# Attention kernel with maxima computed ahead: the first maximum of a plain part moves between the two units of scores

## The reference

```python
q, k, v = (proj(Wq), proj(Wk), proj(Wv))          # 8 heads of 64, 2 sequences of 1024
dots = jnp.einsum('bhqd,bhkd->bhqk', q, k) * scale
attn = jax.nn.softmax(dots, axis=-1)
out = jnp.einsum('bhqk,bhkd->bhqd', attn, v)
```

## Time and profile before

| what | value |
|---|---|
| time, median of 3 runs (lowest to highest) | 388.75 us (388.74 to 388.98) |
| the profiled execution's own time | 388.68 us |
| its span | 386.9 us |
| TensorE busy, matmuls | 378.4 us (98%) |
| TensorE busy, weight loads | 221.9 us (57%) |
| VectorE busy | 274.1 us (71%) |
| ScalarE busy | 276.6 us (72%) |
| GpSimd busy | 293.9 us (76%) |

### The profile page before, as it was taken

One profiled execution on the slowest core, in us unless ns is written; L12 is line 12 of the kernel. 1 busy time (PEld: TensorE's weight loads), 2 busy tenths in 40 slices (PEclk: granted clock), 3 DMA queues, 4 the chain that ended last, 5 costly groups with the idle time before them and its releaser, 6 DMA issues.

```text
span 386.9 us, 6735 instructions
## 1 busy us (share of the span) xinstructions
PE 378.4 (98%) x2368; PEld 221.9 (57%) x2368; DVE 274.1 (71%) x485; ACT 276.6 (72%) x396; POOL 293.9 (76%) x145
## 2 busy tenths in 40 slices
PE   8989999999999999999999999999999999999995
PEld 7856544544555445445544544454456644599995
DVE  6997777787877787777777777877784545766223
ACT  3566656568878887987788687969885589347753
POOL 3080486949999999999999999999999699800021
PEclk9999999999999999999999999999999999999999
DMA  4001002101122041104010710261053105000001
GB/s 138 16 0 36 19 3 56 56 0 56 41 74 56 3 101 12 55 3 110 3 55 5 217 57 1 50 171 57 4 129 93 55 1 160 6 2 15 14 30 54
DMA packets 28245, 19.46 MB, mean 50 GB/s; under 512 B 21264, under 2 KB 23696, under 8 KB 28212
## 3 DMA queue, kind: packets, MB, share of 16 engines
q1 hardware_dynamic: 27636, 18.05, 17.9%
q10 hardware_dynamic: 576, 0.98, 0.8%
HBM read 17.72 MB, written 1.17 MB: 49 GB/s over the span
## 4 chain that ended last, share of the span: by engine, by line
PE 93%; DVE 4%; issue 1%; ACT 1%; DVEq 0%
PE psum L693 31%; PE psum L682 24%; PE psum L620 11%; PE psum L608 6%; PE psum L629 4%; PE psum L737 4%; PE psum L748 3%; PE psum L584 2%; PE psum L704 2%; DVE half_maxes L1127 1%; PE psum L559 1%; PE psum L645 1%; PE psum L647 1%; PE psum L771 1%; PE psum L533 1%
## 5 line engine op out<-in xcount | busy, mean ns | idle before, releaser
L1131 DVE TENSOR_REDUCE half_maxes<-psum 128x1 f32<-128x512 f32 x232 | 148.9, 683 | 26.1 <-PE psum L620 24.5
L894 ACT ACTIVATE probs<-psum 128x1024 f32<-128x1024 f32 x128 | 124.8, 1022 | 54.5 <-PE psum L682 54.1
L693 PE MATMUL psum<-probs,v_all 128*64 128x512 f32 x512 | 123.7, 604 | 0.0
L1360 POOL TENSOR_TENSOR sums<-sums,probs 128x1024 f32<-128x1024 f32 x31 | 74.2, 2395 | 3.7 <-ACT probs L894 3.7
L1360 POOL TENSOR_TENSOR odd_sum<-odd_sum,probs 128x1024 f32<-128x1024 f32 x31 | 74.2, 2395 | 0.0
L693 PEld LDWEIGHTS psum<-probs,v_all 128*64 128x64 f32 x512 | 31.2, 136 | 62.4 <-issue 42.3
L1179 DVE TENSOR_SCALAR psum<-max_plane 128x512 f32<-128x512 f32 (+1 forms) x55 | 43.0, 790 | 31.7 <-ACT probs L894 31.7
L1360 POOL TENSOR_TENSOR sums<-probs 128x1024 f32<-128x1024 f32 x16 | 38.0, 2375 | 27.5 <-ACT probs L894 27.0
L620 PE MATMUL psum<-k_round,q_round 64*128 64x512 f32 x256 | 57.7, 449 | 0.6 <-DVE half_maxes L1131 0.5
L620 PEld LDWEIGHTS psum<-k_round,q_round 64*128 64x128 f32 x256 | 24.1, 183 | 53.5 <-DVE half_maxes L1131 42.9
L682 PE MATMUL psum<-q_round,k_round 64*128 64x512 f32 x256 | 52.4, 404 | 0.1
(11 more groups left out here) (131 smaller groups left out, 450.7 us busy)
## 6 DMA issues: line engine op xcount, KB each, us to landing
max_plane<-rows_scratch SPq DMA_DIRECT2D x16, 512.0 KB, 3.9
inv_sb<-inv_scratch SPq DMA_DIRECT2D x14, 256.0 KB, 5.4
max_rows_of<-maxes SPq DMA_DIRECT2D x128, 0.5 KB, 2.0
v_all<-in_fc SPq DMA_DIRECT2D x4, 512.0 KB, 6.9
fc_late<-in_fc SPq DMA_DIRECT2D x4, 512.0 KB, 6.8
out_h<-probs SPq DMA_DIRECT2D x7, 128.0 KB, 1.8
v_all<-in_w ACTq DMA_DIRECT2D x3, 256.0 KB, 3.6
woT<-in_wo SPq DMA_DIRECT2D x1, 256.0 KB, 3.5
```

The lines of the kernel that those rows point to most:

```text
L693: last = pe.matmul(out_bank[head_rows(h), :], v_all[:, s, kc, head_rows(h)], probs[unit(s, kc, half) % TILES][:, h, :], start=(kc == 0), s ...
L894: last = act.activation(probs[u % TILES][:, heads, :], source, ACT.Exp, scale=SCALE)
L1131: dve.reduce_max(half_maxes[:, h, qc, keys:keys + 1], slot[:, h, :], AX.X).then_inc(maxed, 1)
L1360: pool.tensor_tensor(chain[:, :, :], first[:, :, :], probs[kc][:, :, :], ALU.add).then_inc(own, 1)
```

## The change

In a plain part (two maxima, or none) the first maximum stands between the two units instead of ahead of them, and the second unit's share stands behind the second maximum instead of ahead of it. The lists for the first two parts, for parts with three maxima and for the first part of the last step stay as they are.

```diff
@@ -128,7 +128,7 @@
     elif (s, part) == (STEPS - 1, 0):
         items = maxes[:1] + [first, second] + maxes[1:] + shares[0] + shares[1]
     else:
-        items = maxes[:1] + [first] + shares[0] + [second] + shares[1] + maxes[1:]
+        items = [first] + maxes[:1] + [second] + shares[0] + maxes[1:] + shares[1]
     items += beside_values(s, part)
     items += [("fill", *u) for u in following if u in SCALAR_FILLED]
     if turn > 0:
```

## The result

The changed kernel takes 409.48 us (median of 4 runs, 409.41 to 409.53) against 388.75 us: a ratio of 1.0533, 95% interval 1.0518 to 1.0549. It is 20.7 us slower; the prediction was 411.3 us. The span grew from 386.9 to 407.7 us.

The account below looks back on a forecast made before the run. The prediction took TensorE's own queue, and the releases it waits for, to bound plain parts. Its terms, 14.9 + 4.1 + 2.4 + 1.0 + 0.25 = 22.6 us, on 388.75 us gave 411.3 us, range 404.5 to 416 us.

Parts of the forecast that it names:

- What is moved: In 49 plain parts, only TensorE's queue changes: the first maximum's matmul pair (0.23 us) runs after the first unit's three pairs.
- The ordinary parts: Parts 1, 2, 4, 5, 6 of steps 1 to 6 and step 6's last: +0.48 us in 31, 14.9 us.
- The path: First maximum, VectorE's reduce, bank release, next maximum: 1.30 us against 0.92 us of queued TensorE work, a 0.38 us stall.
- The parts with denominators: Part 3 of steps 1 to 6: the denominator needs the second reduce; +0.68 us in 6 parts, 4.1 us.
- one hand-over for all: From the end of VectorE's reduce to TensorE's next item needing the bank: 0.16 us, for maxima and denominators.
- First parts: Steps 2 to 6: first unit waits for ScalarE's fill, second unit 0.23 us late; +0.48 us in 5, 2.4 us.
- Last parts: Steps 0 to 5: second projection matmul 2.88 us into the part instead of 2.71 us; +0.17 us in 6, 1.0 us.
- Part 5 of step 0: Four pairs in both units: values at 2.77 us instead of 2.52 us, +0.25 us.
- The weights' price: Values follow a maximum that waited after 0.43 us, not 0.32 us: 0.11 us; rival without it 405.9 us, chance 0.06.
- the gain of 0.09 us: Each of six last parts, projections waiting for ScalarE: least gain from the earlier exponential, in the not-slower rival, chance 0.03.
- The rival that stood on the other side: Not slower: release fits into 0.92 us of cover, and the earlier exponential gains 0.8 us; 387.9 us, chance 0.03.
- The rival of the second reduce: VectorE's second reduce decides the release: 0.20 us more in 43 parts, 8.6 us, 419.9 us; chance 0.06.

Follow-up runs that it names:

- the runs with 256 and 128 columns: Changed kernel, VectorE's first reduce of the first maximum reading 256 or 128 of 512 columns in 47 plain parts: 397.27 us and 392.45 us.
- the one-pair kernel: Kernel before, with TensorE issuing the first maximum of the 49 plain parts behind one pair of the first unit's matmuls: 390.31 us.

## Why the prediction was right

**What is moved.** Only TensorE's queue differs between the two kernels; the queues of VectorE, ScalarE, GpSimd and SyncE are the same, item by item, and so the moved share is no change at all. That step held.

**The ordinary parts.** Predicted 0.48 us each. The part shown loses 0.44 us; on average over the 31, from values to values, it is 0.46 us (3.92 us before, 4.38 us after). The path was put at 1.30 us from one place in step 0 and is 1.27 us in the part shown, 1.28 us on average; the first maximum stands at 0.80 us instead of 0.81 us. 31 parts give 14.2 us instead of 14.9 us. The pieces were right: 0.44 us to the reduce, 0.68 us, and 0.15 us to the next maximum.

**The parts with denominators.** Predicted 0.68 us, measured 2.58 us instead of 2.04 us, 0.54 us:

```profile
211.22 0.50 PE L682 MATMUL psum<-q_round,k_round 64*128 64x512 f32 x2
...
212.02 0.40 PE L620 MATMUL psum<-k_round,q_round 64*128 64x512 f32 x2
...
212.46 1.29 DVE L1131 TENSOR_REDUCE half_maxes<-psum 128x1 f32<-128x512 f32 x2 [1.30 <-PE psum L620]
...
213.30 0.50 PE L620 MATMUL psum<-k_round,q_round 64*128 64x512 f32 x2 [0.19 <-DVE half_maxes L1131]
...
213.80 0.16 PEld L704 LDWEIGHTS psum<-sums,ones 128*32 128x32 f32 x8 [0.32 <-DVE half_maxes L1131]
```

The second reduce ends at 213.75 and the denominators start at 213.80, 0.05 us later and not 0.16 us, and so in all 6 parts. The prediction took one hand-over for all; why it is short here, where the wait for a maximum takes 0.14 us with the first and with the second reduce, no run separates. 6 parts give 3.2 us instead of 4.1 us. This is the largest mis-sized term, half of the 1.8 us between 411.3 and 409.5 us; the ordinary parts are most of the rest.

**The first and last parts of the steps.** First parts: the values of the part before start at 117.09 and take 1.87 us, so the part starts at 118.96; its own values start at 121.80, 2.84 us in, against 2.37 us. That is 0.47 us, predicted 0.48 us. Last parts: 2.85 us (111.62 to 114.47) to the second projection matmul against 2.71 us, 0.14 us, predicted 0.17 us. Part 5 of step 0 has 2.73 us (62.22 to 64.95) against 2.51 us before (62.19 to 64.70), 0.22 us, predicted 0.25 us.

The sum with the measured terms, each taken over all its parts, is 14.2 + 3.2 + 2.3 + 0.9 + 0.2 = 20.8 us, beside 20.7 us between the medians and 20.87 us in the middle stretch of the profiles.

**The weights' price.** The 0.11 us behind a maximum that waited is there in the ordinary parts (227.50 to 227.93). By the rule of the Trainium skill that the prediction weighed ("TensorE: Matmul & The Clock Gate", section "Architectural detail: the array is 16× 32×32, not 1× 128×128"), that TensorE's queue can pull weight loads ahead of matmuls in flight, this would have gone. The trace agrees with the rule where nothing is waited for (the weight load of the first maximum starts at 226.00, 0.23 us ahead of its matmul), but behind a wait the load of 227.47 stood only 0.03 us ahead of its matmul, as in step 0.

**What could have given it back.** ScalarE's first exponential does start earlier, 1.00 us into the part (226.43) instead of 1.25 us, and in an ordinary part nothing comes of it. In the last parts the gain of 0.09 us that a rival had read from the rows is real, as the runs with 256 and 128 columns show, but in the changed kernel the stall is larger. The share, forecast for 2.56 us into the part, runs at 2.44 us (227.87), and VectorE builds up no queue. The rival that stood on the other side, a path shorter than 0.92 us, had the right threshold but not the path: only with the reduce cut to 128 of 512 columns does the second maximum come on time, 0.93 us behind the first, and the kernel goes back to 392.45 us.

**The rival of the second reduce was priced too low.** Its 0.20 us more per part is the price of the denominators, which wait for the second reduce themselves. In an ordinary part the second maximum would wait for it, and the values would come another 0.43 us later. With the two reduces in the other order, where the second one does decide, an ordinary part loses 1.06 us and the kernel takes 445.22 us, not 419.9 us. So the measured 409.48 us lies further from this rival than the prediction had it.

## What to carry to other kernels

A step that hands a buffer back has a path: the producer's latency, the consumer's time, the hand-over. Compare it with the work that the producer has queued between the two uses of the buffer, pair by pair; with more cover than path this wait costs nothing, with less each part pays the difference (and here 0.1 us for weights loaded late), whatever the consumer's share of busy time is. Other waits have paths of their own: in five parts the fill by ScalarE cost 0.2 us each even with cover enough. Before moving an item by even 0.7 us in the queue of the busiest engine, look for a place in the old trace where the new order already occurs: here one part of step 0 gave the path within 0.03 us.

## What the runs showed of the hardware

A weight load needs little lead. Where the second maximum's load started 0.14 us ahead of its matmul (210.95 to 211.09, the one-pair kernel) the part had no loss, though the pair's two loads take 0.19 to 0.22 us; with 0.08 us the next item came 0.06 us late (212.92 to 213.00, then 213.38), with 0.03 us it came 0.11 us late (227.47 to 227.50, then 227.93). So the price of exposed weights is not one price but falls with the lead. A reduce of 128 columns took 0.292 us, one of 256 columns 0.425 us and one of 512 columns 0.682 us, which is 1.0 ns per column on top of some 0.16 us.
